# Score maxima from two half-height products side by side in the array, with paired stack loads and the copy of the sums on ScalarE

## What is computed

```python
x = x + xattn(layernorm(x), ctx, pos, Wq, Wkv, Wout, bout)
x = x + ffn(layernorm(x), w_fc, w_proj)

# xattn: 32 heads of 16 columns, 512 queries and 512 keys in each of 4 batches
q = rope((x @ Wq).reshape(b, n, 32, 16)); k, v = split(ctx @ Wkv); k = rope(k)
w = softmax(einsum('bqhd,bkhd->bhqk', q, k) / 4)
attn = einsum('bhqk,bkhd->bqhd', w, v) @ Wout + bout
# ffn: bitlinear(gelu(bitlinear(x, w_fc)), w_proj), where bitlinear normalises and
# quantises its rows and takes the weights as -gamma, 0 or gamma
```

## Time and profile before

| | |
|---|---|
| median of three runs | 771.08 us (770.41 to 771.29) |
| the profiled execution | 771.07 us |
| its span (first to last instruction) | 769.3 us |
| TensorE, matmul records | 754.0 us, 98% of the span |
| VectorE | 661.9 us, 86% |
| ScalarE | 481.9 us, 63% |
| GpSimd | 430.1 us, 56% |
| granted clock of TensorE | 1.00 in each stretch asked for |

### The profile page before, as it was taken

How to read it: one execution, slowest core, us unless ns; L and a number is a source line. 1 busy time by engine, 2 the same in 40 slices (tenths; PEclk the granted TensorE clock), 3 DMA queues, 4 the chain that set the end, 5 groups by cost and what they waited for, 6 DMA issues and landing times.

```text
span 769.3 us, 11882 instructions
## 1 busy us (share of the span) xinstructions
PE 754.0 (98%) x3886; PEld 342.9 (45%) x3886; DVE 661.9 (86%) x927; ACT 481.9 (63%) x830; POOL 430.1 (56%) x501
## 2 busy tenths in 40 slices
PE   5999999999999999999999999999999999999998
PEld 3887877333323322332233223345554455555443
DVE  7888999788888888889888888479998889998895
ACT  4787766787788777788878888765323433333330
POOL 5787776675345446456446557665564845564310
PEclk9999999999999999999999999999999999999999
DMA  8588996555587778887777896326566575544655
GB/s 279 176 219 249 267 260 167 138 141 132 139 170 147 152 157 138 161 179 144 151 162 162 180 192 154 73 69 136 116 135 124 101 147 114 119 96 96 114 106 136
DMA packets 178862, 117.24 MB, mean 152 GB/s; under 512 B 119746, under 2 KB 150514, under 8 KB 178802
## 3 DMA queue, kind: packets, MB, share of 16 engines
q1 hardware_dynamic: 178802, 116.49, 67.6%
HBM read 64.50 MB, written 25.43 MB: 117 GB/s over the span
## 4 chain that ended last, share of the span: by engine, by line
PE 87%; DMA 4%; DVE 2%; ACT 2%; POOL 2%; SPq 1%; issue 1%; POOLq 0%; DVEq 0%; ACTq 0%
PE banks L741 15%; PE banks L725 14%; PE banks L1040 14%; PE banks L1025 14%; PE banks L702 12%; PE banks L297 8%; PE banks L1006 6%; DMA stack_words<-max_rows 2%; PE banks L328 1%; DMA max_rows<-max_parts 1%; PE banks L713 1%; SPq L619 1%; PE banks L280 1%; SPq L257 1%; POOL attn_words L527 0%
## 5 line engine op out<-in xcount | busy, mean ns | idle before, releaser
L815 ACT ACTIVATE probs_words<-banks 128x512 f32<-128x512 f32 x512 | 290.7, 596 | 70.7 <-PE banks L725 57.9
L795 DVE TENSOR_REDUCE maxima<-banks 128x2 f32<-128x1024 f32 x240 | 283.2, 1216 | 41.4 <-PE banks L702 41.4
L725 PE MATMUL banks<-stack_words 98*128 98x512 bf16 x512 | 173.6, 382 | 2.2 <-DMA stack_words<-max_rows 1.2
L702 PE MATMUL banks<-stack_words 96*128 96x512 bf16 x480 | 143.0, 379 | 0.0
L741 PE MATMUL banks<-probs_words,late_words 128*32 128x512 f32 x1024 | 136.4, 605 | 0.0
L725 PEld LDWEIGHTS banks<-stack_words 98*128 98x128 bf16 x512 | 48.7, 96 | 158.0 <-ACT probs_words L815 109.1
L1025 PE MATMUL banks<-ternary_words,late_words 128*128 128x512 f16 x512 | 113.1, 379 | 0.0
L1040 PE MATMUL banks<-ternary_words,stack_words 128*128 128x512 f16 x512 | 112.9, 379 | 0.0
L1224 ACT ACTIVATE probs_words<-probs_words,h_moments 128x2048 f32<-128x2048 f32 (+1 forms) x17 | 32.2, 1901 | 120.6 <-DVE h_moments L1103 120.6
L826 POOL TENSOR_SCALAR neg_max<-maxima 128x16 f32<-128x16 f32 x32 | 8.3, 260 | 145.4 <-DVE maxima L795 145.4
L1025 PEld LDWEIGHTS banks<-ternary_words,late_words 128*128 128x128 f16 x512 | 49.8, 98 | 60.5 <-issue 0.8
(11 more groups left out here) (157 smaller groups left out, 1065.2 us busy)
## 6 DMA issues: line engine op xcount, KB each, us to landing
o_rows<-late_words SPq DMA_DIRECT2D x32, 256.0 KB, 3.4
k_parts<-ternary_words SPq DMA_DIRECT2D x48, 128.0 KB, 3.0
q_parts<-ternary_words SPq DMA_DIRECT2D x48, 128.0 KB, 2.5
stack_words<-q_parts SPq DMA_DIRECT2D x32, 192.0 KB, 3.2
stack_words<-k_parts SPq DMA_DIRECT2D x96, 64.0 KB, 2.7
stack_words<-k_parts SPq DMA_DIRECT2D x32, 192.0 KB, 2.7
attn_words<-in_x_dram SPq DMA_DIRECT2D x16, 256.0 KB, 4.0
probs_words<-in_L_ffn_w_fc_dram SPq DMA_DIRECT2D x16, 256.0 KB, 3.6
```

Of the source, the lines that this page charges most:

```text
L702: mm = self.nc.tensor.matmul(self.score_slot[j % 2][:, i], self.mem.q_stack[0:STACK, slot, head, c * P:(c + 1) * P], self.mem.k_stack[0:ST ...
L725: self.nc.tensor.matmul(self.st_bank[(g * 16 + k) % self.ST_BANKS], self.mem.k_stack[0:STACK + 2, slot, head, c * P:(c + 1) * P], self.mem ...
L795: dve.tensor_reduce(self.maxima[:, g % 2, 2 * j:2 * j + 2], self.score_slot[j % 2], AX.X, ALU.max).then_inc(self.scores_read, 1)
L815: act.activation(self.probs[:, c, head, :], self.st_bank[(g * 16 + k) % self.ST_BANKS], ACT.Exp, scale=1 / math.sqrt(HEAD)).then_inc(self. ...
```

## The change

The maxima are now taken from three of the products of parts in place of six. A main block of 3 x 16 = 48 rows holds them. In heads 0 and 1 of a group (the lower heads) it lies in rows 0 to 47 of the stack, in heads 2 and 3 (the upper heads) in rows 64 to 111. `scores` issues two products of 48 rows for one slot, one of a lower and one of an upper head, for the same chunk of queries, where it issued two products of 96 rows for one head. The program gives these products a tile of 64 x 128 of the array, at row 0 or row 64. The turned product now runs over 114 rows for all heads: six blocks of parts, one block of zeros (rows 96 to 111 in lower heads, rows 0 to 15 in upper heads) and the rows of the maxima at 112 and 113.

Further parts:

- `clear_rows` writes the zero blocks once, with two DMAs in SyncE's step 4; GpSimd sets the zeros they read.
- Stacks are loaded for two groups at a time, and for one half of the heads at a time: 7 DMAs for the lower heads and 8 for the upper ones, of 2 KB pieces where they were of 4 KB. A pair of groups has one semaphore, which is waited for in full (15 DMAs) before the first product of the pair. There is room for three pairs: two in the old place and one in `late_words` (`late_stacks`), which is free only after the projection. `begin_late_stacks` copies the zeros and ones to it with three DMAs.
- The early loads move: both halves of pair 0 in SyncE's step 8, the halves of pair 1 in steps 12 and 14; pair 2 in its attention steps 2 and 3; the halves of pair p from then on in steps 2p-1 and 2p. `turn_max` and `load_max` of group 2 stand in step 4, where they stood in step 3.
- The maxima products run one slot pair ahead (`LEAD = 2`): the first quarter of a step starts with pair 2 of its group, and the last quarter issues pairs 0 and 1 of the next group.
- `save_sums` moves from VectorE to ScalarE, behind the third exponential of the step.
- `keep_running` and `early_scores` use the 48 rows too.

The core of the diff:

```diff
-STACK = 6 * HEAD
+MAIN = 3 * HEAD
+HALF_ROWS = 64
+MAX_ROW = HALF_ROWS + MAIN
+STACK = MAX_ROW + 2
...
-STACK_LOADS = DMA * 7
+STACK_PAIRS = 3
+STACK_LOADS = DMA * (7 + 8)
...
+    def clear_rows(self, sp, rows_set):
+
+        sp.wait_ge(self.row_ones_set, 2)
+        for first, heads in ((STACK - 2 - HEAD, slice(0, 2)), (0, slice(2, 4))):
+            sp.dma_start(self.mem.both_stacks[first:first + HEAD, :, heads].rearrange("p n h c -> p n (h c)").bitcast(F32),
+                         self.row_zeros.unsqueeze(1).to_broadcast([HEAD, 2 * STACK_SLOTS, SEQ])).then_inc(rows_set, DMA)
...
+    LEAD = 2
+    Q_RUNS = (((0, 0, 1), (1, 0, 3), (4, 1, 1), (5, 0, 1)), ((0, 0, 3), (3, 0, 1), (4, 0, 2)))
+    K_RUNS = (((0, 0, 2), (2, 0, 1), (3, 0, 3)), ((0, 2, 1), (1, 1, 1), (2, 0, 1), (3, 0, 2), (5, 0, 1)))
...
+    def load_stacks(self, sp, pair, half):
+
+        mem, g = self.mem, 2 * pair
+        for i in range(2):
+            sp.wait_ge(self.prj.parts_stored[i], PAIR_STORES * (g // HG + 1))
+        need(sp, self.st_ready, (g - 2 * STACK_PAIRS + 2) * 16)
+        for t, where, runs in ((0, mem.q_parts, self.Q_RUNS[half]), (1, mem.k_parts, self.K_RUNS[half])):
+            src = where[g:g + 2].rearrange("g t (d h) c -> (t d) g (h c)", h=GH)
...
+    def wait_stacks(self, pe, g):
+        pe.wait_ge(self.stacks_loaded[g // 2 % STACK_PAIRS], (g // 2 // STACK_PAIRS + 1) * STACK_LOADS)
+
+    def main_product(self, out, g, head, c):
+
+        first = head // 2 * HALF_ROWS
+        rows = slice(first, first + MAIN)
+        return self.nc.tensor.matmul(out, self.stack(0, g)[rows, head, c * P:(c + 1) * P], self.stack(1, g)[rows, head, :],
+                                     start=True, stop=True)
...
-        for i in range(2):
-            c = j % 2 * 2 + i
-            mm = self.nc.tensor.matmul(self.score_slot[j % 2][:, i],
-                                       self.mem.q_stack[0:STACK, slot, head, c * P:(c + 1) * P],
-                                       self.mem.k_stack[0:STACK, slot, head, :], start=True, stop=True)
+        for half in range(2):
+            mm = self.main_product(self.score_slot[j % 2][:, half], g, j // CHUNKS + 2 * half, j % CHUNKS)
         mm.then_inc(self.scores_ready, 1)
...
-        for i in range(count):
-            self.nc.tensor.matmul(bank, self.mem.k_stack[0:STACK, 0, 0, 0:P], self.mem.q_stack[0:STACK, 0, 0, :],
+            self.nc.tensor.matmul(bank, self.mem.k_stack[0:MAIN, 0, 0, 0:P], self.mem.q_stack[0:MAIN, 0, 0, :],
...
-            if s < GROUPS and not begun:
-                self.scores(pe, s, 2 * c)
+            if not begun:
+                self.scores_ahead(pe, ahead)
...
-                if s in (8, 10, 13, 15):
-                    att.load_stacks(sp, (8, 10, 13, 15).index(s))
+                if s == 4:
+                    prj.clear_rows(sp, att.rows_set)
+                if s in EARLY_LOADS:
+                    for half in EARLY_LOADS[s][1]:
+                        att.load_stacks(sp, EARLY_LOADS[s][0], half)
...
-                    if j == 1 and s >= 3:
-                        att.save_sums(dve, s - 3)
...
+                    if k == 2 and s >= 3:
+                        att.save_sums(act, s - 3)
```

More of the change, by code:

```diff
@@ new lines, in stack, with begin_late_stacks @@
+    def stack(self, t, g):
+        return self.stack_pair(t, g // 2)[:, g % 2]
+    def begin_late_stacks(self, sp):
+        late = self.late_stacks.rearrange("p t s h c -> p (t s) h c")
+        for first, heads in ((MAX_ROW - HEAD, slice(0, 2)), (0, slice(2, 4))):
+            rows = slice(first, first + HEAD)
+            sp.dma_start(late[rows, :, heads].rearrange("p n h c -> p n (h c)"),
+                         self.mem.k_stack[rows, :, heads].rearrange("p n h c -> p n (h c)")).then_inc(self.rows_set, DMA)
+        rows = slice(MAX_ROW, MAX_ROW + 2)
+        sp.dma_start(self.late_stacks[rows, 1].rearrange("p s h c -> p (s h) c"),
+                     self.mem.k_stack[rows, 0:2].rearrange("p s h c -> p (s h) c")).then_inc(self.rows_set, DMA)
@@ L778, in tensor_step @@
                 self.scores_turned(pe, turned, 4 * c + 3)
[L779 to L780 removed]
+            if begun:
+                self.scores_ahead(pe, ahead)
+            self.scores_ahead(pe, ahead + 1)
             if rows_meanwhile and 0 <= turned < GROUPS:
```

90 lines of the change are left out of this document (48 added, 42 removed).

## The result

The changed kernel takes **803.21 us**, the median of four runs (800.32 to 804.50), where the kernel before takes 771.18 beside it (median of four): by the means of the runs 1.0404 times as long (95% interval 1.0367 to 1.0441). 764.5 was predicted, in a range that ended at 778. The profiled execution is one of 802.96.

What follows compares the result with a forecast made beforehand. TensorE, with work in 98% of the span, was taken as the bound. From 771.07 us, -18.0, -0.45, -1.8, +3.7, +3.8 and +6.2 summed to 764.5 us; the range was 749 to 778.

Steps and rivals of the forecast that it cites:

- the price of a change of height: On TensorE, switching between full-height and half-height products was taken to cost 0.06 us on either side of a pair.
- Side by side: In the attention, paired half-height products run at once; steps fall from 11.35 to 10.74 us over 29.5 steps: -18.0 us.
- Rival B: A full switch, over 0.075 us a side, leaves pairs at 0.41 of 0.43: 776.9 us, slower; chance 0.27.
- ScalarE's copy: Copy of the sums moved to ScalarE takes 0.565 to 0.59 us; ScalarE then needs 10.13 a step, below TensorE's 10.7.
- Last quarter: The last quarter of step 31 loses its maxima products by the lead and falls to ScalarE's 2.39 us: -0.45 us.
- rows of maxima: TensorE's waits for the row of maxima in the attention, 1.8 us, go because the lead moves the last reduction earlier: -1.8.
- First load: The first maxima product waits for 15 DMAs in place of 7, 3.4 to 4.0 us more: +3.7 us.
- Early maxima products: All 32 are single, half-height products between full ones, paying 0.06 us each side: +3.8 us (0 to 5.8).
- Start of the attention: SyncE's longer queue delays pair 2's loads and group 2's row of maxima; first turned product 6.0 us late: +6.2 (5 to 8).
- Loads in the middle: Second-half stack loads in the attention land in time with cover of 0.3 to 0.5 us: nothing; without cover up to 7.
- The prediction's own mark of being wrong: Among the signs listed as showing the forecast wrong: TensorE waiting for stacks in every other step of the attention.
- Clock: A standing TensorE may get its lower clock; two stops of about 4 us could cost 1 to 3 each, outside the sum.

Runs made afterwards that it cites:

- start_mended: mended, with the third weight block and third row of maxima asked for ahead of SyncE's wait for the last stores of parts: 778.34 us.
- start_and_full_height: start_mended, with the paired maxima products over all 112 rows, one behind the other, nothing side by side: 780.69 us.
- copy_back: The changed kernel with the copy of the sums back on VectorE, ahead of the second reduction of a step: 872.72 us.
- first_half: The changed kernel with the first early product waiting only for the 7 loads of the lower heads, the other 8 issued later: 798.32 us.
- full_singles: The changed kernel with its 32 early single maxima products over all 112 rows in place of 48: 794.74 us.
- weight_behind: The changed kernel with the odd weight load put back behind the write of the maxima in SyncE's step: 793.01 us.
- mended: The changed kernel with full_singles, first_half and weight_behind together, and the loads of pair 2 ahead of the last stores of parts: 778.93 us.
- the three edits: The edits of first_half, full_singles and weight_behind, each made alone on the changed kernel: 798.32, 794.74 and 793.01 us.
- the fourth edit: The part of mended beyond its three single edits: loads of pair 2 ahead of the last stores of parts; not run alone, mended took 778.93 us.
- halves_first: start_and_pairs_together, with second-half loads ahead of the turn of the maxima in even steps and the fourth row of maxima loaded once turned: 795.81 us.
- start_and_pairs_together: start_mended, with the two pairs of maxima products of a quarter behind each other, two changes of height in place of four: 765.31 us.

## Why the prediction was wrong

The step that failed is the price of a change of height, 0.06 where the runs show 0.10; a second one is the loads in the middle of the attention, which were put at nothing and cost about 10 us. Of the 38.7 between 764.5 and 803.2, 15.9 are the term of the side by side, 10.2 the loads in the middle, 4.8 the early single products, 3.3 the first load with the clock behind it, and about 3.5 the two small gains that were not found and the growth behind the milestones.

- **Side by side (-18.0): wrong, and the term that cost the sign.** The switch was taken as 0.06 a side, chosen below the only measured one, 0.09, with the thought that half the height has less to empty. It is 0.10, on either side. Measured: 118 quarters x 0.0175 = -2.1, and 2.4 by the runs start_mended and start_and_full_height. Rival B's mechanism was the right one, even beyond its own price of 0.09. B's own sum is too low by 2.4: with a pair at 0.41 of 0.43 eight pairs save 0.16 in a step, 4.7 in all and not 7.1, which makes 779.3 and lies outside the range. The Trainium skill (TensorEngine Tiling (Array Packing), Key Properties) says that changing the tiling mode drains the engine. The trace agrees for row halves in that each change costs 0.1 us; what fills this time it doesn't show.
- **ScalarE's copy (no cost): right in size** (0.59 at 408.98), but its part in the change was missed: copy_back shows that the lead needs it.
- **Last quarter (-0.45) and rows of maxima (-1.8): not found.** The part behind the milestones grew by 1.3. The waits for rows of maxima did go behind the start (1.2 us of TensorE before, none in start_mended), but three waits for second halves, 1.5 in all, stand there in their place.
- **First load (+3.7): right mechanism, undersized.** The issues took what was foretold (3.9 of 3.4 to 4.0), with a longer landing the product starts 4.3 later, and half clock for the next twelve products adds 2.7. first_half took 4.9 back.
- **Early maxima products (+3.8, 0 to 5.8): undersized, and outside their own bounds.** Each costs 0.27 where 0.12 was taken: 0.2 for its two changes of height and 0.07 that isn't explained. 32 make 8.6, and full_singles took 8.5 back.
- **Start of the attention (+6.2): about right in size, in part by luck.** In the profiled execution no stop for pair 2 is there, and the wait for the row of group 2 is only 0.64, since half clock from 159 to 169 had already slowed TensorE (the first two quarters take 5.0 and 4.1); with it the start costs about 5.3. Seven other kernels of the series have the foretold stop for pair 2, of 2.8 to 4.4, between 169 and 180; in weight_behind it and its half clock make 6.2. In mended, with every other item taken out, the milestones are 340.0 apart: 7.2 over 118 quarters, 5.4 more than before.
- **Loads in the middle (nothing; "up to 7" without cover): wrong.** The cover of 0.3 to 0.5 was worked out without the weight load that the change puts ahead of the loads in odd steps. It waits 3.1 for GpSimd. weight_behind took 10.2 back. The prediction's own mark of being wrong, TensorE waiting for stacks, was to be seen in five steps.
- **Clock ("1 to 3 each", outside the sum): the mechanism was named and left out.** It belongs to each stop as a part of its price.

By the runs: the three edits gave back 4.9 + 8.5 + 10.2 = 23.6, and mended is left with 6.4 over the kernel before (778.93 against 772.51): -2.1 for the pairs, 1.3 behind the milestones and, as what remains, about 7 at the start. That is 30.0 of the 32.0 measured; of the rest 0.7 went with the fourth edit, and 1.3 is the kernel before itself, which took 771.18 beside the change and 772.51 beside mended. In the profiled execution of the change, the 17.2 up to the first milestone are 4.3 and 2.7 of the first load, some 8.4 of single products and 1.1 of half clock from 159, all but 0.7. What share of the stops in the middle is clock rather than waiting isn't separated. How the start would have to be ordered so that no stop is left stays open as well; three orders were tried (mended, start_mended, halves_first), and each moved the stop.

## What to carry to other kernels

Side by side in row halves paid here with two pairs behind each other, and not with single pairs: count the changes of height in the order, give each 0.1 us (a product of half height alone among full ones cost 0.27), and group what is of one height. In a queue that issues every transfer, ask of each moved instruction what it waits for, not only how long it takes to issue; and put a transfer whose end the queue itself waits for ahead of long issues, not behind them. When two edits come together (here a longer lead and a copy on another engine), test whether one holds the other up before pricing them apart.

## What the runs showed of the hardware

- Two products over 48 rows each in different row halves take the time of one (two cover 0.39). Entering and leaving costs 0.09 to 0.10 each: 0.31 to 0.32 between starts where 0.22 is usual. A product of half height alone among full ones cost 0.27 more than one of full height (8.57 a round of three where it was 7.76).
- Behind the first 25 us of a run, every stop of TensorE of 2.2 us or more was followed by the lower clock, 1.2 GHz, for 3.4 to 17.1 us; of those from 1.0 to 2.1 some were (the shortest 1.5) and most were not. Six stretches, 10.2 at 159 in the changed kernel and 3.4 in five others, followed no stop over 0.8, only a row of short ones at the start of the attention. In one of the stretches behind a stop twelve products took 5.42 for 2.76.
- The landing of a turned row, waited for behind seven or eight issues, cost the queue at most 1.8 us at a time (start_and_pairs_together). Waited for with nothing between, it cost 4.3 on average and up to 5.8 (halves_first).
